# Four tiles of surplus blocks run while the last rows are scattered, and the late weights are asked for amid the experts

## The reference

```python
x = x + tanh(g_xattn) * xattn(layernorm(x), ctx)       # x: 8 x 256 x 256, ctx: 8 x 120 x 256
x = x + tanh(g_ffn)   * ffn(layernorm(x))
# xattn: q = x @ W.T + b; softmax(q @ info.T) @ info
# ffn, on N = 2048 tokens of 256:
logits = xf @ expert_sel.T                             # 64 experts
sel_val, sel_idx = top_k(sigmoid(logits), 4)
h = einsum('nd,kde->nke', xf, keys)                    # keys: 64 x 256 x 128
scores = relu(h) * gates[:, :, None]                   # the gate is 0 but for the 4 chosen
out = einsum('nke,kev->nv', scores, values)            # values: 64 x 128 x 256
```

## Time and profile before

| | |
|---|---|
| median of 3 runs | 254.44 us (251.56 to 255.45) |
| profiled execution, own time | 251.02 us |
| its span (first to last instruction) | 249.2 us |
| mean granted PE clock | 0.881 |
| PE busy | 179.5 us (72%) |
| POOL busy | 139.5 us (56%) |
| DVE, ACT busy | 130.3 us, 109.2 us |
| DMA, mean | 265 GB/s, 66.01 MB |

### The profile page before, as it was taken

The page is one execution under the profiler, slowest core; times in us unless marked ns, Lnnn a source line. Parts: engine busy times, 40 slices in busy tenths (PEclk is TensorE's granted clock), DMA queues, the critical chain, the costliest instruction groups (busy, mean ns, idle before and its releaser), DMA issues.

```text
span 249.2 us, 4485 instructions
## 1 busy us (share of the span) xinstructions
PE 179.5 (72%) x1292; PEld 137.3 (55%) x1292; DVE 130.3 (52%) x496; ACT 109.2 (44%) x307; POOL 139.5 (56%) x156
## 2 busy tenths in 40 slices
PE   2999799689576340005999999999999995009773
PEld 2866576466453110005788888887777772007552
DVE  4568899977885752001112122356656561606584
ACT  2677978778766400001445445454545443000111
POOL 4003777777777777600577767777777777700000
PEclk9999999999995555555999999999999999657998
DMA  5899999999999999997589956675567522169996
GB/s 157 241 298 323 355 315 348 370 337 346 321 300 326 346 290 318 367 329 216 170 222 366 312 165 199 209 227 159 170 197 211 163 70 84 66 229 416 395 417 247
DMA packets 40894, 66.01 MB, mean 265 GB/s; under 512 B 5381, under 2 KB 24603, under 8 KB 40864
## 3 DMA queue, kind: packets, MB, share of 16 engines
q1 hardware_dynamic: 32572, 46.68, 60.3%
q0 software_dynamic: 6624, 16.82, 19.4%
q10 hardware_dynamic: 1668, 2.17, 2.4%
HBM read 38.31 MB, written 28.64 MB: 269 GB/s over the span
## 4 chain that ended last, share of the span: by engine, by line
PE 44%; DMA 14%; POOL 13%; DVE 12%; issue 10%; SPq 3%; ACT 3%; POOLq 1%; ACTq 0%; DVEq 0%
PE bank L746 13%; PE bank L775 12%; POOL x_slots L514 11%; DMA keys_sb<-y_rows 7%; PE bank L740 5%; SPq L475 3%; DMA x_slots<-rows,pos_i 3%; POOL y_rows L524 2%; PE bank L556 2%; PE bank L765 2%; PE bank L781 2%; DMA rows<-x_slots 2%; PE bank L628 2%; DVE shared L1288 1%; DMA bq_rows<-in_L_xattn_b 1%
## 5 line engine op out<-in xcount | busy, mean ns | idle before, releaser
L524 POOL DMA_INDIRECT y_rows<-rows,by_place x74 | 73.8, 997 | 39.1 <-ACT rows L1037 21.4
L514 POOL DMA_INDIRECT x_slots<-rows,pos_i x64 | 62.9, 982 | 38.1 <-DVE pos_i L1110 20.2
L1023 ACT COPY xT<-bank 128x512 f32<-128x512 f32 (+1 forms) x38 | 21.8, 574 | 59.3 <-PE bank L740 59.2
L1288 DVE TENSOR_SCALAR shared<-bank 128x256 f32<-128x256 f32 (+1 forms) x38 | 15.9, 417 | 54.9 <-PE bank L746 44.2
L740 PE MATMUL bank<-ident,rows 128*128 128x128 f32 x148 | 22.8, 279 | 20.8 <-DMA rows<-x_slots 20.8
L746 PE MATMUL bank<-xT,keys_sb 128*128 128x128 f32 x256 | 37.5, 288 | 0.0
L746 PEld LDWEIGHTS bank<-xT,keys_sb 128*128 128x128 f32 x256 | 33.1, 195 | 6.2 <-ACT xT L1023 3.3
L775 PE MATMUL bank<-values_sb,shared 128*128 128x256 f32 x128 | 35.1, 391 | 1.2 <-DVE shared L1288 1.2
L740 PEld LDWEIGHTS bank<-ident,rows 128*128 128x128 f32 x148 | 18.0, 146 | 21.7 <-issue 21.7
L1037 ACT COPY rows<-bank 128x512 f32<-128x512 f32 (+1 forms) x38 | 21.8, 575 | 18.2 <-PE bank L775 13.9
L775 PEld LDWEIGHTS bank<-values_sb,shared 128*128 128x128 f32 x128 | 21.4, 190 | 6.6 <-DVE shared L1288 3.1
(11 more groups left out here) (141 smaller groups left out, 300.4 us busy)
## 6 DMA issues: line engine op xcount, KB each, us to landing
x_slots<-values_sb SPq DMA_DIRECT2D x4, 2056.0 KB, 29.9
rows<-x_slots SPq DMA_DIRECT2D x64, 128.5 KB, 4.2
keys_sb<-y_rows SPq DMA_DIRECT2D x16, 512.0 KB, 9.6
values_sb<-in_L_ffn_values SPq DMA_DIRECT2D x5, 1024.0 KB, 13.9
xs<-in_x SPq DMA_DIRECT2D x8, 256.0 KB, 8.3
out<-xs ACTq DMA_DIRECT2D x7, 256.0 KB, 6.2
values_sb<-in_L_ffn_values SPq DMA_DIRECT2D x1, 1408.0 KB
rows<-x_slots SPq DMA_DIRECT2D x40, 32.1 KB
```

The lines of the kernel that those rows point to most:

```text
L514: pool.indirect_dma_start(x_slots, bass.IndirectOffsetOnAxis(ap=pos_i[:, t * K + k:t * K + k + 1].bitcast(U32), axis=0), rows[:, t % RB * ...
L524: pool.indirect_dma_start(y_rows, bass.IndirectOffsetOnAxis(ap=result_at[:, t:t + 1], axis=0), y_sb[:, t % R, :], None, bounds_check=last_ ...
L1023: act.copy(xgT[:, 2 * ring + part.start:2 * ring + part.stop, :].rearrange("p u d -> p (u d)"), pT(place_of(part, ring))[:, part.start * D ...
L1288: dve.tensor_scalar(hidT[:, 2 * ring + part.start:2 * ring + part.stop, :].rearrange("p u n -> p (u n)"), pH(place_of(part, ring))[:, part ...
```

## The change

Sixteen surplus blocks, four quads, are put ahead of everything (`EARLY` = 4 tiles, pairs 0 and 1). Once the ranks of tile 12 are known (`EARLY_T`), DVE notes how many rows of each expert have landed by then, for experts 0 to 39. Blocks that lie wholly in those rows are "early", the others "late". The tables are made in two rounds: `early_rows` and `early_experts` first, then the rest. SP and ACT each load two of the four blocks of each early tile, once the padding and the scatters up to tile 12 have landed. The early tiles use places of `rows` that tiles 11 to 13 have left; ACT waits for the scatters of tiles 12, 13 and 14 before it overwrites theirs. The two last early quads have their keys copied to `keys_early`, in the place of late values. PE and ACT then go on with pair 2, the first e tile's; the number of tiles stays 74 and of quads 10, and the mixed part is now `"eeeqeeeqeeeqeee"` twice. Pair 0 is no longer cut in halves.

SP no longer issues late keys or values before the rows. ACT asks for keys 40 to 47, 48 to 55 and 56 to 63 after the results of pairs 3, 5 and 7, and for values 50 to 60 after pair 9; SP asks for the other 13 values after its first 20 e tiles and after the early quads have used `keys_early`. `late_in` now counts six loads. The reads of `y_rows` use four semaphores instead of 16, and read t waits until read t - 4 has landed.

```diff
     RB = 5
     R = 10
     ALONE = 40
-    MIXED = "eeqeeqeeeqeeqeeqe" * 2
+    EARLY = 4
+    EARLY_T = 12
+    MIXED = "eeeqeeeqeeeqeee" * 2
     GROUPS = 2
-    TILES = ALONE + len(MIXED)
-    QUADS = MIXED.count("q")
+    TILES = EARLY + ALONE + len(MIXED)
+    QUADS = EARLY + MIXED.count("q")
     GE, GQ = (MIXED.count(kind) // GROUPS for kind in "eq")
     V = 2
-    REST = 25
+    REST = 30
     RING = 3
     PAIRS = R // 2
     UNITS = N * K // H - Q * Q
+    PLACES = UNITS + Q * EARLY
     SPARE = Q * (QUADS + REST * V)
     PAIR = 2 * M
     PT = 2 * TB
     ADDED = (1, 3, 6, 8, 10, 12, 14)
     LATE = 24
     FREE_KEYS, FREE_VALUES = 56, (50, 61)
-    LATE_LOADS = 5
+    LATE_LOADS = 6
...
+        keys_early = late_values[:, 0:2 * Q * C * F].rearrange("p (n a f) -> p n a f", n=2, a=Q)
+        assert 2 * Q * C * F <= (FREE_VALUES[0] - E + LATE) * D
...
-        yg_in = [sem(f"yg_in{t}") for t in range(T)]
+        yg_in = [sem(f"yg_in{i}") for i in range(4)]
...
+            if t < EARLY or t >= TILES:
+                return "q"
+            return "e" if t < EARLY + ALONE else MIXED[t - EARLY - ALONE]
...
+        EARLY_PAIRS = EARLY // 2
+
+        def place_in(t):
+
+            return (t + Q) % R
...
-            return min(p + 2 + (p > 5), TILES // 2)
+            return min(p + 2 + (p > EARLY_PAIRS + 5), TILES // 2)
...
-            return min(p + 1 + (p > 9), TILES // 2)
-
-        def parts_of(p):
-
-            return [slice(0, 1), slice(1, 2)] if p == 0 else [slice(0, 2)]
-
-        def place_of(part, ring, last=RING - 1):
-
-            return last if part.start else ring
+            return min(p + 1 + (p > EARLY_PAIRS + 9), TILES // 2)
...
+        def early_block_rows(eng):
+
+            return nc.values_load_multi_w_load_instructions(
+                early_rows[0:1, 0:Q * EARLY], engines=[eng.engine], min_val=0, max_val=E * PITCH - P,
+                skip_runtime_bounds_check_because="they are slots of the expert or the padding in front")[1]
+
+        def early_block_experts(eng):
+
+            eng.wait_ge(r_early, 2)
+            experts = nc.values_load_multi_w_load_instructions(
+                early_experts[0:1, 0:Q * EARLY], engines=[eng.engine], min_val=0, max_val=E - 1,
+                skip_runtime_bounds_check_because="they are sums over one expert's number at most")[1]
+            return [experts[Q * n:Q * n + Q] for n in range(EARLY)]
...
-            late_keys_in(FREE_KEYS, E)
-            late_values_in(*FREE_VALUES)
-            sp.wait_ge(a_S, T)
-            late_keys_in(E - LATE, FREE_KEYS)
+            sp.wait_ge(padded, 16 * E // FE)
+            sp.wait_ge(r_early, 1)
+            first_blocks = early_block_rows(sp)
+            for n in range(RB):
+                sp.wait_ge(scattered[n], 16 * K * len(range(n, EARLY_T + 1, RB)))
+            for t in range(EARLY):
+                load_blocks(t, first_blocks[Q * t:Q * t + Q // 2])
             sp.wait_ge(a_O, T)
-            sp.wait_ge(padded, 16 * E // FE)
             sp.wait_ge(r_first, 1)
             first_rows = rows_at(alone_rows[0:1, 0:2 * R], 2 * R)
             for n in range(RB):
                 sp.wait_ge(scattered[n], 16 * K * len(range(n, T, RB)))
             for first in range(0, 2 * R, R):
                 turn_alone(first, first_rows[first:first + R])
-            late_values_in(E - LATE, FREE_VALUES[0])
-            late_values_in(FREE_VALUES[1], E)
+            sp.wait_ge(e_Q, EARLY)
+            late_values_in(sp, E - LATE, FREE_VALUES[0])
+            late_values_in(sp, FREE_VALUES[1], E)
...
             for t in range(T):
-                sp.dma_start(yg[:, t, :], y_tiles[:, t, :]).then_inc(yg_in[t], 16)
+                after(sp, yg_in[t % 4], t // 4, 16)
+                sp.dma_start(yg[:, t, :], y_tiles[:, t, :]).then_inc(yg_in[t % 4], 16)
...
-            pe.wait_ge(r_units, 1)
+            pe.wait_ge(r_units, 2)
             pe.matmul(end_ps, upto[0:E, 0:E], units_bf[:], start=True, stop=True).then_inc(r_end, 1)
-            pe.matmul(total_ps, ones_bf[0:E, 0:1], units_bf[:], start=True, stop=True).then_inc(r_end, 1)
-
-            pe.wait_ge(r_unit, 1)
-            pe.matmul(lead_ps, lead[:], unit_of[:], start=True, stop=True).then_inc(r_block, 1)
-            pe.matmul(expert_ps, expert_col[:], unit_of[:], start=True, stop=True).then_inc(r_block, 1)
+            pe.matmul(total_ps, ones_bf[0:E, 0:E], units_bf[:], start=True, stop=True).then_inc(r_end, 1)
+
+            for n in range(2):
+                pe.wait_ge(r_unit, 2 * n + 2)
+                pe.matmul(lead_ps, lead[:], unit_of, start=n == 0, stop=False, skip_group_check=True).then_inc(r_block, 1)
+                pe.matmul(expert_ps, expert_col[:], unit_of, start=n == 0, stop=False,
+                          skip_group_check=True).then_inc(r_block, 1)
...
+            def early_rows_of(p):
+                pe.wait_ge(e_Tc, 2 * p + 2)
+                for u in range(2):
+                    quad = 2 * p + u
+                    quad_rows(u, p, At(quad), keys_early[:, quad - 2, :, :] if p else None)
+
+            def early_turned(p):
+                for u in range(2):
+                    mm = quad_turned(u, p, At(2 * p + u))
+                mm.then_inc(e_H, 2)
+
+            def early_results(p):
+                pe.wait_ge(e_h, 2 * p + 2)
+                after(pe, e_y, 2 * (p - 1))
+                for u in range(2):
+                    mm = result_quad(u, p, p % 2, At(2 * p + u))
+                mm.then_inc(e_Y, 2)
+
             pe.wait_ge(c_Mc, len(units))
             pe.wait_ge(r_table, TABLE)
-            pe.wait_ge(scattered[(T - 1) % RB], 16 * K * len(range((T - 1) % RB, T, RB)))
-            def hidden_rows(n, part):
-                if n == ALONE // 2:
+            slots_T(At(0), 0)
+            slots_T(At(1), 1)
+            early_rows_of(0)
+            early_turned(0)
+            early_rows_of(1)
+            early_results(0)
+            early_turned(1)
+            early_results(1)
...
+            def rows_landed(t):
+
+                act.wait_ge(scattered[t % RB], 16 * K * len(range(t % RB, t + 1, RB)))
+
+            act.wait_ge(padded, 16 * E // FE)
+            act.wait_ge(r_early, 1)
+            first_blocks = early_block_rows(act)
+            for n in range(RB):
+                act.wait_ge(scattered[n], 16 * K * len(range(n, EARLY_T + 1, RB)))
+            for t in range(EARLY):
+                for a in range(Q // 2, Q):
+                    act.dma_start(xg[a * H:(a + 1) * H, place_in(t), :],
+                                  x_slots[ds(first_blocks[Q * t + a], H), :]).then_inc(xg_in[t // 2], 16)
+            rows_out(At(0), 0)
+            act.wait_ge(e_Q, 2)
+            quad_rows_out(At(0), 0, 0)
+            quad_rows_out(At(1), 0, 1)
+            rows_out(At(1), 1)
+            rows_landed(EARLY_T)
+            results_out(At(0), 0)
+            act.wait_ge(e_Q, 4)
+            quad_rows_out(At(2), 1, 0)
+            quad_rows_out(At(3), 1, 1)
+            rows_landed(EARLY_T + 1)
+            results_out(At(1), 1)
+            rows_landed(EARLY_T + 2)
+
+            rows_out(At(EARLY_PAIRS), EARLY_PAIRS % RING)
...
+                if p == EARLY_PAIRS + 1:
+                    act.wait_ge(a_S, T)
+                    late_keys_in(act, E - LATE, (E - LATE + FREE_KEYS) // 2)
+                if p == EARLY_PAIRS + 3:
+                    late_keys_in(act, (E - LATE + FREE_KEYS) // 2, FREE_KEYS)
+                if p == EARLY_PAIRS + 5:
+                    late_keys_in(act, FREE_KEYS, E)
+                if p == EARLY_PAIRS + 7:
+                    late_values_in(act, *FREE_VALUES)
...
+                if s - 3 == EARLY_T:
+                    dve.scalar_tensor_tensor(out=on_diag[:], in0=rank_ps[0:E, :], scalar=float(P - (H - 1)),
+                                             in1=ident[0:E, 0:E], op0=ALU.add, op1=ALU.mult).then_inc(r_landed, 1)
+                    dve.wait_ge(r_landed, 1)
+                    dve.tensor_reduce(early_at[0:ALONE], on_diag[0:ALONE, :], AX.X, ALU.add).then_inc(r_landed, 1)
...
+            own(dve.tensor_scalar(count_i[:, 2:4], count_i[:, 0:2], H.bit_length() - 1, None, ALU.logical_shift_right))
+            own(dve.tensor_copy(units_f[:], count_i[:, 2:4]))
+            own(dve.tensor_tensor(early_f[:], units_f[:, 0:1], units_f[:, 1:2], ALU.subtract))
+            dve.tensor_copy(units_bf[:, 0:1], early_f[:]).then_inc(r_units, 1)
+            dve.tensor_copy(units_bf[:, 1:2], units_f[:, 1:2]).then_inc(r_units, 1)
+            dve.wait_ge(r_end, 2)
+            own(dve.tensor_copy(unit_end[:], end_ps[:, 0:1]),
+                dve.tensor_tensor(unit_start[:], end_ps[:, 0:1], early_f[:], ALU.subtract))
+            own(dve.tensor_scalar(done, iota_f[0:E, :], unit_end[:, 0:1], None, ALU.is_ge),
+                dve.tensor_tensor(lead_from[:], unit_start[:], units_f[:, 1:2], ALU.subtract))
```

(33 more changed lines are left out.)

259 lines of the change are left out of this document (119 added, 140 removed).

## The result

The changed kernel takes 260.8 us (median of 6 runs, 257.0 to 264.4), the kernel before beside it 253.5 (6 runs, 251.6 to 255.9): a ratio of 1.0215, with an interval of 1.0128 to 1.0302. It is slower, by 7.3 us in the medians, where 2.7 us less was forecast. In two more comparisons of the same pair the ratio was 1.033 (medians, of two executions only) and 1.0287. Medians here are of all executions of a kernel, while a ratio with an interval leaves out those in the chip's slower state, to which the profiled execution of the change, the longest of its six, belongs.

What follows compares the result with a forecast made beforehand. POOL's scatters were taken to bound the experts. Early chain -3.7, fewer quads -0.4, ACT's issues +0.6, late weights +0.5, y_rows reads +0.3 gave -2.7: 251.7 us from a median of 254.44, range 246.5 to 260.

Steps and rivals of the forecast that it cites:

- What bounds the kernel: Stretch of experts: POOL's scatters, one per 1.277 us, bound it within 2.5 us; PE just ahead; y_rows reads DMA-bound.
- When the early blocks can start: Start of stage two: padding ends last at 97.1, loads from 99.0, pair 0 in at 103, pair 1 at 105.3.
- The early chain: Early pairs on PE, DVE, ACT: pair 2's first scatter at 122.0 instead of 125.67, 3.7 us gained.
- ACT's four issues: Stretch of experts: four large DMA issues at 0.86 us each on ACT, 0.6 us lost (0 to 10).
- The late weights: Amid the experts: 6.3 MB in 167 GB/s free, landed at 162.4; 0.5 us lost (0 to 12).
- Reads with four in flight: Last stage, reads of y_rows: bandwidth stays, as 2 MB outstanding exceed a landing; 0.3 us lost (0 to 1).
- (b): Amid the experts: late weights become the bound, DVE waiting at its quads below 165 GB/s free; 259.3 us, chance 0.20.
- (c): Early chain: PE's clock stays at half, pair 2's scatter at 126; 255.7 us, chance 0.12.
- (d): Early tiles: early places not filled, an extra pass runs; about a pair of tiles more, 257 us, chance 0.02.
- the bad end: Late weights' upper end: at 290 GB/s with keys, 90 to 100 left for half the bytes, landing at 175.

Runs made afterwards that it cites:

- Both cuts: The change with SP's 13 late values in seven small loads, 253.8 us; and the change with ScalarE's late keys in twelve small loads, 254.5 us.

## Why the prediction was wrong, point by point

- *What bounds the kernel* held: in the change POOL runs at its pace up to the hole, PE catches up behind it, from 191.85 POOL's pace is the chain again, and the hole cost its length.
- *When the early blocks can start*: right. The padding ended last, at 96.35 (97.1 forecast); the early loads went out at 98.1 on both queues (99.0); PE started at 102.67 (103), and pair 1's rows were in at 105.05 (105.3).
- *The early chain*: right in its number, pair 2 at 121.68 against 122.0, and less so inside. First result at 112.89 (113.4). The clock was at 0.50 until 110, rose, and fell to 0.57 again between 114 and 118, where one value product of 16 took 1.89 us; I had full clock from 109. Key products cost less than taken (1.91 us for two quads at half clock, 2.4 to 2.6 forecast), so the errors met in part. Forecast gain 3.7, shown 4.0. Counted from the first scatter of stage one (21.90 before, 23.13 after) it is 5.2. Seven other profiles with this early part on quiet chips had pair 2 between 119.4 and 124.0, six of them 97.3 to 99.5 us behind that first scatter (98.6 in the change, 103.8 before). But the late loads moved alone, without early tiles, had it after 97.9. The forecast took it that the late weights' absence ahead of the last scatter "is hidden"; in that kernel the last scatter landed after 2.67 us instead of 6.40 and the first rows after 2.10 instead of 4.20, and the gain was there without one early block. So that 4.0 met 3.7 doesn't show that early tiles gained it: they may have added nothing to what the moved loads give. The time agrees, 1.029 for the late loads alone with free reads, 1.0287 for the change with four in flight (which cost 0.5%).
- *ACT's four issues*: right. 0.82, 0.75, 0.76 and 1.63 us where 0.86 each was taken, and POOL lost at most 0.4 us over the three of keys. No issue was held on ACT's side in the change.
- *The late weights*: here it failed, in two sentences. "The ten tiles of rows that SP has in flight can be put off meanwhile (1.3 MB, 8 us), which speaks for an earlier end": I took rows as traffic that comes first and late weights as what fills the free 167 GB/s, landing at 162.4. But the rows got no precedence. The 6.3 MB landed from 123.51 to 154.4, at 204 GB/s, SP's queue fell to 129 GB/s, and the rows of pair 12 took not 8 us but 21.0 from request to landing, 13.0 of them past PE's need. And "The wait of SP for the early quads' keys stands behind 20 row loads: nothing" costed the wait and not the 1.7 MB behind it, which stand ahead of every later row. The term was +0.5 (0 to 12); it measured +14 in the profile, and its wait was 11.3 and 12.2 us in the profiles of the repeat and of the late loads alone. Its upper end was near, but at another place: I looked for the stall at DVE's register load of the quads near 161, and this came at PE's transposes of pair 12.
- *Why before had no hole* though SP asked for the same 13 values in the same place: the other 11 experts' values and the keys were asked for by 97.0, in the dead time ahead of PE's start, and from 117 to 119 the DMA share was down to 0.10 and 0.07. The 13 alone are 1.7 MB, 5 us at the earlier trace rows's 368 GB/s and 7 at the 247 of SP's own queue, well within the lead of five pairs. With ScalarE's 4.6 MB on the second queue they no longer are: at the 129 GB/s that SP's queue then moved they take 13 us. The Trainium skill (DMA: Bandwidth & Descriptors, "Queues, rings and completion order") has each DMA engine go round the queues that have work, packet by packet. The trace agrees in that no queue starved and SP's fell from 247 to 129 GB/s when ScalarE's had work; how long each turn is was not measured. Both cuts fit: one takes the bytes ahead of the rows away, the other those of the neighbour. The Trainium skill (DMA: Bandwidth & Descriptors, "Issuing engines are not separate DMA queues") says that a second issuing engine saves only the sequencer's time. Here moving 1.7 MB from one to the other took the ratio from 1.0287 to 0.9933 and PE's wait from 11.3 us or more to none; for a small load that follows, what stands ahead in its own queue counts.
- *Reads with four in flight*: +0.3 taken, 1.4 measured in the kernel before. "2 MB outstanding are 5 us of DMA time, more than a landing" does not hold as it stands: a read's landing takes 6.4 us there (the median after). Whether the gap is all of the 1.4 was not tried. In the profiled run the stage lost 2.5.
- *Rivals*. (b) had the right part, late weights with DMA full, and the wrong victim; its price of 259.3 is near the 260.8 measured, its point of decision (165 GB/s free, DVE waiting) played no part. (c) was half there, and pair 2 came at 121.68 nonetheless. (d) did not occur: 74 scatters, as forecast.
- The sum with measured terms, in the profiled spans: -4.0 (early chain, with the later stage one in it) + 14.9 (hole of 14.2, the slow pairs behind it, less small gains) + 2.5 = +13.4, from 249.2 to 262.6. Of the medians the change costs 7.3, about half of that, so the single terms are those of one long execution.

## What to carry to other kernels

When bulk loads are moved from dead time into a busy stage, don't ask first whether their bytes fit in the free bandwidth, but how many bytes stand ahead of the next small load, in its own queue and, by turns, on the others; that time has to be shorter than the lead of the engine that needs it. Cut the bulk into parts of about one small load each and lay them between the small ones, or put it on a queue on which nothing urgent follows. Here that turned +2.9% into -1.8%, and -2.65% with the reads let go, each against the kernel before on its own chip.

And when a change has two parts, price each of them alone. Here the gain that was forecast for one part, to a few tenths of a microsecond, was there with the other part alone.

## What the runs showed of the hardware

- The issue of a row load on SP (128 KB) took 0.33 us usually. It took 9.11 us behind 1.7 MB on its own queue with ScalarE's loads beside them, 6.79 in the kernel with the late loads alone, and 2.6 in the repeat of the change, with a longer landing (14.43 instead of 11.87). The issue of an early block's load took 10.29 us with 4.6 MB asked for ahead of it. No later issue of SP's went out meanwhile.
- SP's queue moved 129 GB/s beside ScalarE's and POOL's (the change, 130 to 150), and 247 beside POOL's alone (before, 127.3 to 140, DMA full from 130).
- Row loads that took 2.10 us to land in a quiet stretch (share 0.45, late loads alone) took 10.0 to 14.4 with the DMA share at 1.04 to 1.10. The kernels with small parts had landings of 10.0 and 10.6 us among them, and 1.2 and 0.4 us of waits for rows on PE in all, as rows were asked for five pairs (13 us) ahead.
- Two of the chips gave about 300 us for kernels that take 250 on others, with 3 to 7 us at a time in which an engine waited for nothing visible. The change was slower there too, but its hole was only 3.6 us long.
- Keys and values loaded at 342 to 372 GB/s together beside rows and scatters, whichever queue asked. Why the window of the earlier trace rows on which I based the bad end had only 290, with a DMA share of 1.00, was not tried.
